# Recommender tower on one core: coarser holds for the last gathers, and transposes moved behind layer 1

## What is computed

```python
e = jnp.stack([tbl_f[ids[:, f]] for f in range(26)], axis=1)     # 512 x 26 x 128
sd = jnp.einsum('bfd,bd->bf', e, dense)                          # dots with the dense vector
ss = jnp.einsum('bfd,bgd->bfg', e, e)                            # dots of all pairs
z = jnp.concatenate([dense, sd, ss[:, iu, ju]], axis=1)          # iu, ju: pairs with f < g
h = jnp.concatenate([z, dense], axis=1)                          # 607 columns
h = jnp.maximum(h @ W_top1 + b_top1, 0.0)                        # 512 hidden
h = jnp.maximum(h @ W_top2 + b_top2, 0.0)                        # 256 hidden
y = h @ W_top3                                                   # one number a sample
```

## Time and profile before

| what | value |
|---|---|
| the three runs | 134.86, 135.13, 139.09 us (median 135.13) |
| span of the profiled execution, first to last instruction | 131.6 us |
| the profiled execution's own time | not listed apart from the three; against the median, 3.5 us lie around the span |
| PE busy | 109.4 us (83%) |
| POOL busy | 64.3 us (49%) |
| DVE, ACT busy | 80.8 us, 65.6 us |
| D0 ends, D1 starts, D1 ends | 66.1, 72.9, 84.2 us |
| D2 starts, D2 ends | 98.1, 102.1 us |
| D3 starts | 111.4 us |

### The profile page before, as it was taken

How to read it: one execution, slowest core, us unless ns; L and a number is a source line. 1 busy time by engine, 2 the same in 40 slices (tenths; PEclk the granted TensorE clock), 3 DMA queues, 4 the chain that set the end, 5 groups by cost and what they waited for, 6 DMA issues and landing times.

```text
span 131.6 us, 2789 instructions
## 1 busy us (share of the span) xinstructions
PE 109.4 (83%) x1086; PEld 95.1 (72%) x1086; DVE 80.8 (61%) x218; ACT 65.6 (50%) x150; POOL 64.3 (49%) x66
## 2 busy tenths in 40 slices
PE   6999999199999998857798257990699997999794
PEld 6767888078868887947797146980669995999691
DVE  5799998798897999903088030385310886088101
ACT  4676560892975598503089300360730894087411
POOL 8477875675886778757167735276520000000000
PEclk9999999959999999996899977998569999999999
DMA  3987985359989812121102201021110000000000
GB/s 116 255 232 178 246 255 134 111 164 278 299 225 284 270 50 59 40 60 32 35 22 60 59 26 42 22 62 40 40 40 5 0 0 0 5 5 0 0 0 1
DMA packets 5030, 12.35 MB, mean 94 GB/s; under 512 B 1725, under 2 KB 1853, under 8 KB 5018
## 3 DMA queue, kind: packets, MB, share of 16 engines
q1 hardware_dynamic: 2906, 8.15, 21.2%
q0 software_dynamic: 1920, 3.94, 11.6%
q10 hardware_dynamic: 192, 0.10, 0.3%
HBM read 12.18 MB, written 0.00 MB: 93 GB/s over the span
## 4 chain that ended last, share of the span: by engine, by line
PE 65%; DVE 12%; issue 11%; ACT 6%; another core or an unknown queue 4%
PE dots L465 28%; PE dots L512 15%; DVE pairs L361 9%; PE hidden L537 4%; ACT pairs L299 4%; PE turned L492 4%; PE last_layers L441 2%; PE last_layers L554 2%; PE hidden L554 2%; PE dots L435 2%; PE last_layers L561 2%; PE turned L537 2%; PE last_layers L474 1%; DVE onehot L368 1%
## 5 line engine op out<-in xcount | busy, mean ns | idle before, releaser
L260 POOL DMA_INDIRECT rows<-tbl,gather_idx x60 | 61.6, 1027 | 31.7 <-issue 15.2
L361 DVE COPY pairs<-dots 27x128 f32<-27x128 f32 (+8 forms) x88 | 23.8, 270 | 21.1 <-PE dots L512 18.5
L299 ACT COPY pairs<-dots 27x128 f32<-27x128 f32 (+8 forms) x88 | 21.0, 238 | 29.0 <-PE dots L512 27.0
L368 DVE TENSOR_SCALAR onehot<-ids_h 125x512 fp32r<-125x512 f16 x88 | 33.0, 431 | 2.9 <-PE dots L465 2.0
L465 PE MATMUL dots<-onehot,high 125*128 125x512 f32 (+1 forms) x88 | 33.7, 401 | 0.0
L465 PE MATMUL dots<-onehot,low 125*128 125x512 f32 (+1 forms) x88 | 31.8, 380 | 0.1
L512 PE MATMUL dots<-embT 128*64 128x54 f32 x512 | 20.1, 241 | 8.5 <-issue 7.8
L512 PEld LDWEIGHTS dots<-embT 128*64 128x64 f32 x512 | 18.8, 155 | 10.4 <-issue 10.2
L313 ACT CAST high<-table 125x1024 fp32r<-125x1024 f32 (+1 forms) x12 | 11.7, 979 | 15.9 <-PE dots L465 12.6
L465 PEld LDWEIGHTS dots<-onehot,low 125*128 125x128 f32 x88 | 16.8, 193 | 3.7 <-DVE low L376 0.7
L465 PEld LDWEIGHTS dots<-onehot,high 125*128 125x128 f32 x88 | 17.0, 193 | 3.2
(11 more groups left out here) (46 smaller groups left out, 78.3 us busy)
## 6 DMA issues: line engine op xcount, KB each, us to landing
table<-tbl SPq DMA_DIRECT2D x10, 448.0 KB
wp<-w_pairs SPq DMA_DIRECT2D x2, 512.0 KB
rows<-tbl,gather_idx POOLq DMA_INDIRECT x60
table<-tbl SPq DMA_DIRECT2D x10, 52.0 KB
wd<-w_dense SPq DMA_DIRECT2D x1, 512.0 KB
w2s<-w SPq DMA_DIRECT2D x1, 512.0 KB
table<-tbl SPq DMA_DIRECT2D x2, 224.0 KB
denseT<-dense_t SPq DMA_DIRECT2D x1, 256.0 KB
```

Of the source, the lines that this page charges most:

```text
L260: pool.indirect_dma_start(out=rows[:, t % 2, n, :], out_offset=None, in_=tables[GATHERED_TABLES[n]][:, :], in_offset=bass.IndirectOffsetOn ...
L299: return nc.scalar.copy(dst, src)
L361: return nc.vector.tensor_copy(dst, src)
L368: nc.vector.tensor_scalar(onehot[:, i % 2, c, :], ids_h[:, i, :], float(c), None, ALU.is_equal).then_inc(onehot_ready, 1)
```

## The change

Two things. First, the holds of the late gathers: gather 40 still waits for D0, 46 to 51 now wait for D1, and 52 to 59 for D2. The holds by turned batches 10 to 12 and by layer 1 are gone, as is the hold of gather 51 on its own. Second, in `STEPS` of the stage behind D2: B3.1 goes from ahead of L1.0 to behind C2.1, B3.2 goes from ahead of M1 to behind it, and B3.3 from ahead of Y1 to behind it.

```diff
--- before.py
+++ after.py
@@ -57,7 +57,7 @@
     GATHERS_AHEAD, GATHERS_PER_TABLE = 4, 3
 
     LATER_GATHERS = GATHERS_AHEAD + GATHERS_PER_TABLE * (N_ONEHOT + 1)
-    HELD_BY_DOTS, HELD_BY_BATCH, HELD_BY_LAYER1 = {40: 1, 51: 2}, {46: 10, 48: 11, 53: 12}, {55: 1, 57: 2}
+    HELD_BY_DOTS = {40: 1, 46: 2, 52: 3}
     WARMING = 29
     WARMING_BETWEEN = 6
     CHUNKS1 = HIDDEN1 // 128
@@ -179,7 +179,7 @@
             T0 T1 B0.0 T2 B0.1 T3 B0.2 T4 B0.3 T5 B1.0 T6 T7 B1.1 T8 B1.2 T9.0 B1.3 T9.1 T9.2
             T10.0 B2.0 T9.3 T9.4 D0 C0.0 T10.1 T10.2 T10.3 T10.4 C0.1 P0 B2.1 P1 W14 B2.2
             D1 C1.0 B2.3 L0.0 L0.1 R0 C1.1 B3.0 M0 Y0
-            D2 C2.0 B3.1 L1.0 L1.1 R1 C2.1 P2 B3.2 M1 B3.3 Y1
+            D2 C2.0 L1.0 L1.1 R1 C2.1 B3.1 P2 M1 B3.2 Y1 B3.3
             D3 C3.0 L2.0 L2.1 R2 C3.1 P3 M2
             L3.0 Y2 L3.1 R3 M3 Y3""".split()]
 
@@ -251,10 +251,6 @@
                         pool.wait_ge(table_selected, (k - GATHERS_AHEAD) // GATHERS_PER_TABLE)
                     if k in HELD_BY_DOTS:
                         pool.wait_ge(dots_done, HELD_BY_DOTS[k])
-                    if k in HELD_BY_BATCH:
-                        pool.wait_ge(transposed, HELD_BY_BATCH[k])
-                    if k in HELD_BY_LAYER1:
-                        pool.wait_ge(layer1_done, HELD_BY_LAYER1[k])
                     if t >= 2 and n % BATCH_T == 0:
                         pool.wait_ge(transposed, batch_no(t - 2, b) + 1)
                     pool.indirect_dma_start(
```

## The result

The changed kernel takes 138.44 us (median of 5 runs, 136.91 to 143.77). The kernel before takes 135.04 us beside it. The ratio is **1.0229, with a 95% interval of 1.0142 to 1.0316**: slower, though the interval doesn't settle whether by more or less than 2%. I had forecast 134.1 us and a gain of 1.0 us. The measured time lies inside my range, on its far side.

The account below looks back on a forecast made before the run. Bound by the chain of D steps, with PE results stalled until gathers in flight are through. Span 131.6 - 5.1 - 1.5 + 5.6 = 130.6 us, with 3.5 around it 134.1 us; 8-in-10 range 128.8 to 139.7.

Parts of the forecast that it names:

- Gathers 46 and 47 leave D1: In D1: the stall on B2.2 ends at 74.7 to 75.2 us instead of 77.7, minus 5.1 us (3.8 to 5.4).
- D1 to D2: Stage between D1 and D2, with gathers 46 to 51 behind D1: a gain of 1.5 us, between 0.5 and 5.3.
- first end: Between D1 and D2: B3.0 stalls to the end of the gathers, D2 starts at +13.4, a gain of 0.5.
- Gathers 52 to 59 behind D2: Between D2 and D3: eight gathers delay D3, a loss of 5.6 us: the 3.5 floor plus 2.1 for stall or clock.
- floor of 12.8: Behind D2: B3.3 waits for the last gather's rows, so D3 can't start before +12.8, a loss of 3.5 us.
- The stages behind D3 ... keep their 20.3 us: From D3's start to the end: no gather is issued now or then, so the 20.3 us stay.
- third stage: Between D2 and D3, with eight gathers behind D2: plus 5.6 us, or 5.1 by the clock alone.
- The 3.5 us around the span: Whole run: 3.5 us between the profiled span and the median, added to the forecast span of 130.6 us.
- first term: In D1: gathers 46 and 47 leave it, the stall on B2.2 ends earlier, minus 5.1 us.
- second rival: Behind D2: a stall lasts across all eight gathers, 139.7 us; its sign, B3.1's placing later than +10 us; chance 0.18.
- A stall across all eight gathers: At B3.1 behind L1, before D3: release only at +11.3, 10.2 us lost there, 139.7 us, slower; chance 0.18.
- The stalls aren't the gathers': B2.2 stalls until 77.7 us as now, D1 to D2 keeps 13.95 us, late rows cost 3.5 to 5.1: 139 us; chance 0.12.

Follow-up runs that it names:

- quick chip: Both kernels rerun unchanged on another chip, without stalls: before 117.13 and 115.27 us (medians of two batches), changed kernel at ratios 1.0482 and 1.0479.
- quiet POOL: Changed kernel with gather 46 held until L0.1 is done instead of D1, so no gather is in flight during D1, B2.3 and L0: 140.0 us.
- plain loads: Changed kernel with gathers 45 to 52 as SP loads of fixed rows plus ten more loads: 120.92 and 118.92 us without stalls, 135.42 us on chip 12.
- three more gathers: Changed kernel with three extra gathers, into a buffer nobody reads, directly behind gather 51: 143.57 us, one run.
- added products: Changed kernel with 30 small products on zeros between Y1 and B3.3, written where nothing reads: 138.15 and 139.35 us.

## Why the prediction was wrong

The sign was wrong: spans +3.5 us where I had summed -1.0. Step by step:

*"Gathers 46 and 47 leave D1": mechanism right, too large.* The release came at 75.18 us (forecast 74.7 to 75.2). But the 122 records that were left took 5.33 us instead of my 3.7, because the clock fell all the same (0.77 over D1). On chip 13 the same 122 records took 3.82 us, so this part varies from one execution to the next. I had named this end, 80.4 us, and taken 79.0, "since the array is fed again before it has been idle as long as now". D1 ended at 80.27: -3.9, not -5.1. On the quick chip the term is zero.

*"D1 to D2", minus 1.5: wrong.* "In return L0.1 comes out ahead of the wait" is the sentence that failed. L0.1 itself is held to +8.8, and with M0 at half clock D2 starts at +13.69, beside the first end's +13.4. That gathers are what holds it, the runs show: a quiet POOL gives +4.1, plain loads +4.05, three more gathers +11.0.

*"Gathers 52 to 59 behind D2", plus 5.6: the size came out by luck, from other parts.* The floor of 12.8 is the quick chip's 13.06. On the first chip that floor doesn't bind: B3.3 waits for DVE to place B3.2, not for gather 59. The 15.09 us there are the new order's own 11.7, 2.2 us by which L1's ReLU is late, and 1.2 us behind B3.2's entry (4.44 us to D3 instead of 3.28), where M1's result is late and B3.3 runs slowly, in 0.87 us. "Moving them costs nothing as long as rows come last" failed: the chain through B3.1's placing is 2.4 us longer than the 9.30 of before, and it is this chain that a stall lengthens. I had placed the stall at B3.1, behind L1, with M1 and B3.2 waiting for it, at +17.4; it sat on L1 itself, and was released at +5.97, amid the gathers.

*"The stages behind D3 ... keep their 20.3 us": wrong*, by 1.8 us. I had put the halved clock of D3 into the price of the gap, as an alternative to the stall, though D3 lies behind the gap and the two add. The third stage with D3 costs 5.8 + 1.8 = 7.6, where I had taken 5.6 for both. The Trainium skill, "TensorE: Matmul & The Clock Gate", section "HAM oscillation — how this bites in real kernels", was the warning for it. The traces agree in part. D3 takes 5.2 to 6.6 us in seven of the nine traces that have the new order, gathers behind D2 and no added products (clock 0.65 and 0.69 in two of the windows above). But it takes 3.94 us in the run with the quiet POOL, whose gap is longer, and 5.49 us in the run without the hold at 52, whose gap is only 11.71.

*The 3.5 us around the span* are 1.8 us around a span in every run (136.91 - 135.1, 138.44 - 136.6) and 1.7 us by which the profiled execution of before was quicker than the median (an estimate: 131.6 + 1.8 = 133.4). The changed kernel's profiled one stands 1.5 us below its median, so this term did no harm.

Of the misses, 1.2 + 1.2 + 0.2 + 1.8 and 0.1 ahead of D1 are the 4.5 us between -1.0 and +3.5.

*The signs.* Those for the first term came: POOL's idle time filled by D1, DVE's start at 75.18, and no gap in D1 from then, for 5.1 us. B3.3 came 13.3 us behind D2's end, not 11 to 11.5. B3.1's placing on ACT, at +9.5, stayed just short of the +10 that I had named for the second rival.

*The rivals.* "A stall across all eight gathers", at 139.7 against 138.44, had the direction and half of its mechanism: M1's release came 1.9 us behind gather 59, but L1's came amid the gathers, and the gap is 15.09, not 17.4 or more. "The stalls aren't the gathers'", at 139, is nearest in number only. On the first chip B2.2's release moved to 75.18, and although the second stage kept its length, 13.69 against 13.95, the runs with a quiet POOL and with plain loads, on chips 3 and 12, show such a hold to be the gathers' doing. Yet on the quick chip it is the true account of this kernel (nothing from the first two terms, plus 3.8, plus D3's clock), and there the change costs the most (1.0482 and 1.0479). The Trainium skill, "SBUF — State Buffer", section "Who interferes with whom", has "DMA never contends with a compute engine". The plain loads agree with it, in the one run where this could show. POOL's gathers beside L0, at +8.8 against +4.05, don't fit it as it stands, though no run shows that it is their transfers, and not another part of POOL's work on them; on the quick chip nothing speaks against it.

What stays open: the way in which POOL's gathers hold back PE's results, why the quick chip lacks it, and how long one result is held within a stretch of gathers. Results came from 2.6 us behind the end of the last gather to 9 us before it, and the ReLU on layer 1 came at +8.8 with six, seven and eight gathers alike. "Until the gathers in flight are through" is thus not the mechanism. A stall with a length of its own would fit the +8.8, but not the +11.0 with nine. What decides whether D3 runs slowly stays open too.

## What to carry to other kernels

Moving transfers from one stage to a later one only pays if the later stage has cover for their full serial length: eight gathers at 1.25 us each, between one D step and the next, lengthened that gap from 9.30 to 13.06 us on the chip where nothing else happened. When steps are moved, work out the new order's own chain first: here it was 11.7 us, and every delay on it came on top. Add the clock of the step behind an idle time to the price of that idle time; the two are not alternatives. When a cure seems to cost time, look whether the loss lies ahead of it or behind it. And when a stall is blamed on a neighbour, test it by silencing the neighbour and by putting a different one in its place, on more than one chip.

## What the runs showed of the hardware

- One kernel, before, takes 115 to 117 us (medians) on one chip and 135 to 138 us on the others tried. D1 to D2 is 8.50 us there against 13.95 on the first chip, with the same work on PE, DVE and ACT; D2 to D3 is 9.30 us on both.
- On the chips with stalls, results of products come late beside POOL's indirect DMAs: the ReLU on layer 1 at +3.8 to +4.1 us without, +8.8 in most traces with six to eight (but +6.0 and +7.4 in two with eight), +8.1 amid fourteen, +11.0 with nine. Plain loads at 93 GB/s did nothing, in one execution.
- POOL issues one gather of 128 rows each 1.25 us (0.94 us busy, 0.30 us between).
- The time of a run is its span and 1.8 us, in all runs.
